# An addition ahead of each indirect transfer of the first retention stage, and the keys' half sums moved from GpSimd to VectorE

## The reference

```python
h = tok(x, conv_w)                 # each token's three rows of a table of 8000 x 3 x 128, one for each tap;
                                   # the taps are added with shifts by one token
h = h + retention(layernorm(h))    # xpos-rotated queries and keys, decay mask, group norm, 8 heads
h = h + experts(layernorm(h))      # 8 experts, each token goes to its best two
h = h + complex_retention(layernorm(h))
h = h + merged_ffn(layernorm(h))
```

## Time and profile before

| | us |
|---|---|
| median of three runs (2256.82 to 2259.97) | 2257.84 |
| the profiled execution | 2260.11 |
| its span, first to last instruction | 2258.1 |
| TensorE busy, share of the span | 2006.5, 89% |
| VectorE | 1469.5, 65% |
| ScalarE | 1340.2, 59% |
| GpSimd | 1123.3, 50% |
| mean granted TensorE clock | 0.937 |

### The profile page before, as it was taken

One profiled execution on the slowest core, in us unless ns is written; L12 is line 12 of the kernel. 1 busy time (PEld: TensorE's weight loads), 2 busy tenths in 40 slices (PEclk: granted clock), 3 DMA queues, 4 the chain that ended last, 5 costly groups with the idle time before them and its releaser, 6 DMA issues. The chain is left out here.

```text
span 2258.1 us, 57460 instructions
## 1 busy us (share of the span) xinstructions
PE 2006.5 (89%) x19420; PEld 1513.2 (67%) x19420; DVE 1469.5 (65%) x4372; ACT 1340.2 (59%) x2844; POOL 1123.3 (50%) x1242
## 2 busy tenths in 40 slices
PE   4888878878878759999999968999999799999997
PEld 2555545555555547777777755777777589999997
DVE  3766666766767533333333337999999668888877
ACT  3655655555556322222222217999999589988985
POOL 4466566566555458887787862112112014333434
PEclk9998998989889769999999988999999899999999
DMA  2111111112111035555555641311110001111111
GB/s 80 55 54 54 58 55 55 55 54 60 51 53 47 29 105 167 166 163 163 161 160 158 164 136 49 132 41 37 46 37 28 6 25 39 44 39 39 39 48 39
DMA packets 113820, 168.88 MB, mean 75 GB/s; under 512 B 19235, under 2 KB 66748, under 8 KB 113573
## 3 DMA queue, kind: packets, MB, share of 16 engines
q1 hardware_dynamic: 87940, 105.22, 16.6%
q0 software_dynamic: 25760, 62.09, 8.6%
HBM read 121.92 MB, written 45.32 MB: 74 GB/s over the span
## 5 line engine op out<-in xcount | busy, mean ns | idle before, releaser
L344 POOL DMA_INDIRECT sent<-a_xn_mid,a_pos_cur x256 | 250.8, 980 | 94.1 <-issue 72.5
L1252 ACT ACTIVATE b_hT<-b_hbank,b_w 128x512 f32<-128x512 f32 (+1 forms) x156 | 98.3, 630 | 320.1 <-PE b_hbank L1222 267.3
L1196 POOL DMA_INDIRECT done<-b_y,b_row x270 | 264.2, 979 | 48.1 <-issue 43.7
L1232 PE MATMUL b_bank<-b_w,b_hT 128*128 128x128 f32 x2160 | 254.2, 275 | 0.9 <-DVE b_hT L1278 0.9
L1278 DVE TENSOR_SCALAR b_hT<-b_hbank,b_w 128x512 f32<-128x512 f32 (+1 forms) x156 | 105.7, 677 | 226.6 <-PE b_hbank L1222 206.4
L1232 PEld LDWEIGHTS b_bank<-b_w,b_hT 128*128 128x128 f32 x2160 | 247.5, 192 | 1.1 <-DVE b_hT L1278 1.1
L1222 PE MATMUL b_hbank<-b_xT,b_w 128*128 128x512 f32 (+1 forms) x624 | 247.2, 539 | 0.8 <-ACT b_xT L1259 0.8
L1485 POOL TENSOR_TENSOR c_k_early<-c_xn,c_k_decay 64x512 f32<-64x512 f32 x32 | 40.8, 1276 | 340.2 <-ACT c_xn L1692 340.2
L450 PE MATMUL a_bank<-a_wkkv,a_xT 128*128 128x384 f32 x256 | 122.4, 563 | 98.0 <-issue 86.3
L744 DVE TENSOR_TENSOR a_masked<-a_scores,a_tabs 128x1024 f32<-128x1024 f32 x128 | 154.7, 1220 | 45.9 <-remote 26.8
L1222 PEld LDWEIGHTS b_hbank<-b_xT,b_w 128*128 128x128 f32 x624 | 113.4, 192 | 87.5 <-issue 83.1
(11 more groups left out here) (245 smaller groups left out, 4728.9 us busy)
## 6 DMA issues: line engine op xcount, KB each, us to landing
b_w<-pack_dram SPq DMA_DIRECT2D x78, 258.0 KB
b_w<-pack_dram SPq DMA_DIRECT2D x78, 256.0 KB
c_rows<-done SPq DMA_DIRECT2D x32, 512.0 KB, 3.9
b_x<-sent SPq DMA_DIRECT2D x57, 260.0 KB
d_b_all<-b_rows SPq DMA_DIRECT2D x32, 256.0 KB, 3.4
out_dram<-h_all SPq DMA_DIRECT2D x32, 256.0 KB, 2.3
b_b<-pack_dram SPq DMA_DIRECT2D x78, 64.5 KB
tv<-tv_dram SPq DMA_DIRECT2D x1, 4736.0 KB, 16.0
```

What stands on the lines that cost most here:

```text
L344: pool.indirect_dma_start(out=sent_d, out_offset=bass.IndirectOffsetOnAxis(ap=pos_cur[:, g.par, b, k:k + 1], axis=0), in_=xn_mid[:, g.par, ...
L1196: pool.indirect_dma_start(out=done_d, out_offset=bass.IndirectOffsetOnAxis(ap=row[:, s.k, j:j + 1], axis=0), in_=y[:, s.par, j, :], in_off ...
L1232: m = nc.tensor.matmul(y_bank[s.par][:, j * D:(j + 1) * D], hT[:, c, j * P:(j + 1) * P], w[:, s.par, W2 + c * D:W2 + (c + 1) * D], start=( ...
```

## The change

Three edits, all of them in `retention_phase`:

1. Each indirect transfer of the stage, gather or scatter, gets a small addition ahead of it on GpSimd: x + x into x, for 128 x 128 words of a stripe of `tv`, the buffer for a table that is loaded in a later stage and is set to zero here. Each addition waits for the one before by a semaphore (`pool_step` for scatters, `ids_step` for gathers; the copy of the indices counts on the latter too).
2. `k_sum` moves from GpSimd, where it stood between the gathers and the scatters, to VectorE, between `place_tokens` and the third mask. Its size and inputs stay. `q_sum` stays on GpSimd.
3. The `sem_inc` of `pool_step` at the head of each group's scatters goes; at the end GpSimd waits for the last addition of each chain.

```diff
@@ retention_phase, gpsimd
             def gather(g):
                 p = g.par
-                pool.wait_ge(ids_ready, g.n + 1)
+                pool.wait_ge(ids_step, g.n * (GB + 1) + 1)
                 if g.is_past(2):
                     pool.wait_ge(h_ready, g.n - 1)
                 take_ids(g.after())
                 for b in range(GB):
+                    space_out(spare[:, 1, :], ids_step, g.n * (GB + 1) + (b + 2))
                     pool.indirect_dma_start(
             def scatter(g, parts):
-                if 0 in parts:
-                    pool.wait_ge(placed, g.n + 1)
-                    pool.sem_inc(pool_step)
                 for i in parts:
                     b, k = divmod(i, 2)
+                    if i == 0:
+                        pool.wait_ge(placed, g.n + 1)
+                    space_out(spare[:, 0, :], pool_step, g.n * (2 * GB) + (i + 2))
                     pool.indirect_dma_start(
-            def k_sum(g):
-                pool.wait_ge(krot_ready, g.n + 1)
-                if g.is_past(1):
-                    pool.wait_ge(kcen_ready, g.n)
-                pool.tensor_tensor(kx[:], kv[:, g.par, :, 0:D], kv[:, g.par, :, D:2 * D], ALU.add).then_inc(kx_ready, 1)
+            def space_out(x, step, n):
+                pool.wait_ge(step, n)
+                pool.tensor_tensor(x, x, x, ALU.add).then_inc(step, 1)
@@ gpsimd, step
                 if g := s.at(3):
                     gather(g)
-                if g := s.at(1):
-                    k_sum(g)
                 if g := s.at(-2):
-                    scatter(g, range(0, GB))
+                    scatter(g, range(GB))
+            pool.memset(spare, 0.0).then_inc(pool_step, 1)
@@ vector
+            def k_sum(g):
+                dve.wait_ge(krot_ready, g.n + 1)
+                if g.is_past(1):
+                    dve.wait_ge(kcen_ready, g.n)
+                v.tensor_tensor(kx[:], kv[:, g.par, :, 0:D], kv[:, g.par, :, D:2 * D], ALU.add).then_inc(kx_ready, 1)
@@ vector, step
                 if g := s.at(-2):
                     place_tokens(g)
+                if g := s.at(1):
+                    k_sum(g)
                 if g := s.at(0):
                     mask(g, 1, 0)
@@ build
+            spare = tv[:, 0:2, :]
```

More of the change, by code:

```diff
@@ L122, in retention_phase @@
 def retention_phase(nc, h_all, w_all, routing, sent_d, ids_d, table_d, wq_d, wqs_d, wkkv_d,
-                    gn_w_d, gn_b_d, tabs_d, tabs_c_d, gate_w_d, gate_c_d, slot_c_d, tags_d):
+                    gn_w_d, gn_b_d, tabs_d, tabs_c_d, gate_w_d, gate_c_d, slot_c_d, tags_d, spare):
     with ExitStack() as ctx:
@@ L235, in retention_phase @@
         consts = sem("consts")
-        ids_ready = sem("ids_ready")
+        ids_step = sem("ids_step")
         tok_made = sem("tok_made")
@@ L321, in take_ids @@
                 pool.tensor_copy(cur_ids[:, g.par * GB:(g.par + 1) * GB],
-                                 ids[:, bass.ds(g.n * GB, GB)]).then_inc(ids_ready, 1)
+                                 ids[:, bass.ds(g.n * GB, GB)]).then_inc(ids_step, 1)
             def gather(g):
                 p = g.par
-                pool.wait_ge(ids_ready, g.n + 1)
+                pool.wait_ge(ids_step, g.n * (GB + 1) + 1)
                 if g.is_past(2):
@@ L367, in step @@
                     gather(g)
-                if g := s.at(1):
-                    k_sum(g)
                 if g := s.at(-2):
-                    scatter(g, range(0, GB))
+                    scatter(g, range(GB))
             pool.memset(ids[:, NB:], 0).then_inc(pool_step, 1)
+            pool.memset(spare, 0.0).then_inc(pool_step, 1)
             pool.wait_ge(ids_loaded, 16)
-            pool.wait_ge(pool_step, 1)
+            pool.wait_ge(pool_step, 2)
             take_ids(Group(0, 0, 0))
@@ L379, in _ @@
                 pool.wait_ge(scattered[i], (NG // 2) * (2 * GB) * 16)
+            pool.wait_ge(pool_step, NG * (2 * GB) + 2)
+            pool.wait_ge(ids_step, NG * (GB + 1) + 1)
         @block.tensor
@@ L2954, in build @@
                        routed.enter_context(nc.sbuf_tensor("ident_b", [P, P], F32)))
+            spare = tv[:, 0:2, :]
             retention_phase(nc, h_all, w_all, routing, sent, a["ids"].bitcast(U32), a["table"], a["wq"],
                             a["wqs"], a["wkkv"], a["gn_w"], a["gn_b"], a["tabs"], a["tabs_c"], a["gate_w"],
-                            a["gate_c"], a["slot_c"], a["tags"])
+                            a["gate_c"], a["slot_c"], a["tags"], spare)
             experts_phase(nc, routing, sent, done, a["pack"], a["fill_tags"])
```

## The result

The changed kernel takes **2198.68 us** in the median (2195.18 to 2203.28), beside 2257.33 of the kernel before in the same comparison: ratio 0.9739, 95% interval 0.9719 to 0.9759. It is faster, as forecast, but 38.7 us above the predicted 2160, and just above the range's end of 2198. The profiled execution spans 2197.6 us, 60.5 less than before. All of it lies in the first stage: the MEMSET that opens the next one stood at 821.59 and stands at 760.4 now.

A forecast was written before the change was run, and what follows sets the result against it. A chain between engines, lengthened by late TensorE signals, was taken to bound the 23.74 us step; 20.4 us a step saves 90, the tail 8, the head 0: 98 off 2260.1 gives 2162, median 2160 us, range 2136 to 2198.

The forecast's parts named there:

- the hold: First retention stage: TensorE's signals arrive late while GpSimd issues indirect transfers in a row; removal taken as -5.0 us a step.
- The rival by which the spaced transfers still hold (2334): First stage: spacing does not break the hold, gate's signal comes later, +2.8 us a step, 2334 us; chance 0.06.
- The chain without holds with k_sum on VectorE: Full step's chain between engines: 23.74 less 5.0 gives 18.7, plus 0.7 for k_sum, 19.4 us.
- The term for k_sum itself: k_sum on VectorE, counted on the chain's path: +0.7 us a step.
- GpSimd's own step: GpSimd in a full step: twelve spaced transfers at 1.54 us plus 1.55 for q_sum, copy and gaps, 20.0 us.
- two other limits near: Full step: the chain's 19.4 and the ring's 20.3 us beside GpSimd's 20.0, so 20.4 was taken.
- The rival with 0.21: First stage: GpSimd's additions and VectorE's two-input operations block each other, 21.3 us a step, 2184 us, up to 2198; chance 0.21.
- What was late next: Full step after the change: GpSimd becomes the bound at 20.0 us, the chain right under it at 19.4.
- The ring of tok and gathers: First stage: a gather is read by tok one step later; 40.6 us for two steps, 20.3 each.
- Tail and head: Ends of the first stage: tail net -8 us (0 to -14), head net 0 (-2 to +1).
- The signs by which I meant to tell: Profile afterwards: gate sum's wait under 1.5 us if right; q_sum 21 us or more apart, spacers much over 0.37 if wrong.
- The half clock: TensorE granted 0.50 of its clock from 408.06 to 414.89 us, mid-step; to be gone or shorter afterwards.

The follow-up runs named there:

- chip B: One of the four chips of the follow-up runs: the kernel before took 2272.71 us there, the changed kernel 2197.61.
- chips A and D: Two of the four follow-up chips: the kernel before took 2108.52 and 2111.84 us on the first, 2107.77 on the second, where the changed kernel took 2200.54.
- k_sum-only kernel: The kernel before with k_sum moved to VectorE and no additions: 2117.03 us (ratio 1.0041) on chip A, 2229.03 (0.9851) on chip C.
- chip B's pair: Changed kernel plus one 1024-column VectorE operation a step: addition with two SBUF inputs 2218.10 us, reduction with one 2203.28, beside 2197.61.
- the k_rotate cut short: Changed kernel with k_rotate on VectorE cut from 1024 columns to 32: 2180.08 us, beside the changed kernel's 2200.54 on chip D.
- chip C: One of the four follow-up chips: the kernel before took 2258.35 us there; the changed kernel was not run on it.

## Why the prediction came out as it did

**The bound and the hold: right, on the chips that have it.** The wait before the gate sum was to fall from 4.2 to the undisturbed 0.8 us a step; it is 0.84. "Remote" waits are gone, and neither the masks nor the sum that closes the retention (L815, now L822) has a wait left among the listed ones (1.0 and 0.9 us a step before). The rival by which the spaced transfers still hold (2334) is refuted by the 0.13 us above, and by the other 26 gates with it. What the hold costs was sized right: 5.0 us a step and 12 in the tail make 27 x 5.0 + 12 = 147 us, and the kernel before takes 146 to 150 us less on chips without it (2257.8 - 2107.8 = 150.0, 2257.8 - 2111.8 = 146.0); against chip B's 2272.7 it is up to 165. The sum took it for the kernel's property, which no single trace could contradict. So the forecast that the change is faster was right for a kind of chip and not for the kernel, and that the result was timed on the kind of chip that the trace came from was luck: on chips A and D the same reasoning would have met a slowdown.

**The chain without holds with k_sum on VectorE: right.** 19.4 us forecast, 19.27 in the k_sum-only kernel on chip A (about 19.0 at its median time, which is 6.4 us under the profiled one). The term for k_sum itself was too high: 0.7 a step, while that kernel is 8.5 us slower than before, 0.3 a step.

**GpSimd's own step: the step that failed.** It was 12 x 1.54 + 1.55 = 20.0, taken as 20.4 with two other limits near; it is 21.83. The timeline of one step shows both parts of the error (GpSimd, 393 to 416 us, the rows that differ and some that don't):

```profile
393.38 1.27 POOL L359 TENSOR_TENSOR a_qx<-a_qa,a_qb 128x512 f32<-128x512 f32 x1
...
394.86 0.40 POOL L353 TENSOR_TENSOR tv<-tv 128x128 f32<-128x128 f32 x1
...
400.10 1.77 POOL L333 DMA_INDIRECT a_rows<-table_dram,a_cur_ids  x1 [0.16 <-issue]
401.89 0.56 POOL L353 TENSOR_TENSOR tv<-tv 128x128 f32<-128x128 f32 x1
...
403.64 0.41 POOL L353 TENSOR_TENSOR tv<-tv 128x128 f32<-128x128 f32 x1
404.22 1.00 POOL L345 DMA_INDIRECT sent<-a_xn_mid,a_pos_cur  x1 [0.17 <-issue]
405.24 0.65 POOL L353 TENSOR_TENSOR tv<-tv 128x128 f32<-128x128 f32 x1
...
407.08 0.41 POOL L353 TENSOR_TENSOR tv<-tv 128x128 f32<-128x128 f32 x1
...
408.67 0.41 POOL L353 TENSOR_TENSOR tv<-tv 128x128 f32<-128x128 f32 x1
...
410.83 1.26 POOL L345 DMA_INDIRECT sent<-a_xn_mid,a_pos_cur  x1 [0.17 <-issue]
...
415.30 1.28 POOL L359 TENSOR_TENSOR a_qx<-a_qa,a_qb 128x512 f32<-128x512 f32 x1
```

Undisturbed, a spaced scatter goes from 407.08 to 408.67, 1.59 us, and a spaced gather, not shown, 1.55 to 1.57 in the same step. I had 1.54, from the experts' addition of 192 columns and a slope of 0.0023 us a column; that slope came from the 512 columns of q_sum, and the addition takes 0.41, not 0.38. With q_sum and the copy at 394.86 - 393.38 = 1.48 the undisturbed step is 8 x 1.59 + 4 x 1.56 + 1.48 = 20.4, **0.4 over** the sum.

The rest is VectorE's. In this step the fourth gather takes 1.77 us instead of 0.96, one scatter 1.26 instead of 0.99, two additions 0.65 and 0.56 instead of 0.41, together 1.47; over all steps the means give 12 x (0.466 - 0.410) = 0.67 for the additions and 8 x (1.020 - 0.979) + 4 x (1.054 - 0.965) = 0.68 for the transfers (0.965 is the gathers' mean in the kernel before; 0.979 in the earlier trace rows). **1.35 us a step**. 20.4 + 1.35 = 21.8. The base of the scatters can be taken otherwise: from the 0.99 that an undisturbed one takes in this step it is 1.27 instead of 1.35, and q_sum's waits for VectorE, 3.1 us in 24 steps, are the 0.13 that is then left. VectorE's rows at the long ones show what ran:

```profile
399.71 1.32 DVE L776 TENSOR_TENSOR a_kv<-a_kv,a_tabs 128x1024 f32<-128x1024 f32 x1
...
401.51 0.68 DVE L792 TENSOR_TENSOR a_kx<-a_kv 128x512 f32<-128x512 f32 x1
...
404.96 0.68 DVE L802 SCALAR_TENSOR_TENSOR a_kcen<-a_ksum,a_kx 128x512 f32<-128x512 f32 x1
...
410.46 0.77 DVE L816 TENSOR_TENSOR a_kn<-a_kcen,a_krs 128x512 f32<-128x512 f32 x1
```

k_rotate starts at 399.71, the gather at 400.10, and it ends 0.84 us after k_rotate's end at 401.03, nearly a gather's whole 0.96, as if it had begun in earnest only then. k_sum, which the change itself brought to VectorE, runs to 402.19 and covers the start of the addition at 401.89, 0.15 too long. k_center starts at 404.96 and the addition at 405.24 is 0.24 too long. The scaling of the keys, 410.46 to 411.23, covers the start of the long scatter at 410.83. The operations named have two inputs in SBUF. That each meeting is the cause of its delay is read from these overlaps; that VectorE's operations of this kind set GpSimd's lengths is shown by chip B's pair and by the k_rotate cut short, which moved 0.4 and 0.66 us of the step. VectorE pays too: k_rotate's mean is 1354 ns over these steps and 1210 with additions of 64 columns, where the meetings fall otherwise:

```profile
L776 DVE TENSOR_TENSOR a_kv<-a_kv,a_tabs 128x1024 f32<-128x1024 f32 x28 | 37.9, 1354 | 0.0
```

```profile
L776 DVE TENSOR_TENSOR a_kv<-a_kv,a_tabs 128x1024 f32<-128x1024 f32 x29 | 35.1, 1210 | 0.0
```

(the first row is the changed kernel's, the second that of the 64 columns on chip D)

**The rival with 0.21 was the mechanism, with too small a price.** It gave each addition 0.07 us by meetings (0.9 a step, 21.3) and named k_rotate, k_center, the scaling and k_sum. Additions came out at 0.056 each, so that estimate was fair. What it missed is that the transfers themselves, 1.0 us long and two thirds of GpSimd's time, meet VectorE as well, for as much again. Forecast 2184 to 2198; measured 2198.7. Its argument against itself, that L1814's median is untouched, was weak: there 61 additions of GpSimd stand beside its 128 executions in 400 us, so most of them can meet none. The Trainium skill, SBUF — State Buffer, Who interferes with whom, states the rule (two SBUF inputs on VectorE against a reading GpSimd instruction, the second blocks). The additions agree with it in kind: those of 0.65 and 0.56 us instead of 0.41 end 0.25 and 0.26 us after the operation of VectorE that they meet, which is less than a whole addition. On the transfers it says that a tensor_tensor was not seen to stall DMA, and infers why; here gathers behind k_rotate took 1.77 instead of 0.96 and cutting k_rotate brought their mean from 1056 to 1005 ns, more than halfway to the 965 of the kernel before, so by the measurement they are stalled, the indirect ones of this kernel at least. Whether it is their reading of the indices or something else that waits was not separated.

**What was late next: right in kind.** GpSimd is the bound. The ring of tok and gathers shows as TensorE's 2.5 us a step of waiting, but it adds nothing of its own: GpSimd's instructions and its waits for VectorE make up the 21.83, and it waits for TensorE nowhere.

**Tail and head: near.** 60.5 us less in the span, 27 x (23.74 - 21.83) = 51.6 of them from the full steps, so 8.9 from both ends, against the 8 forecast. **The sum with the measured step**: 2160 + 27 x (21.83 - 20.4) = 2198.6, and 2198.7 was measured, so the whole miss lies in that one term. **The range** had its upper end at that rival's worst case and should have held more, since both mis-sized terms pushed the same way.

**The signs by which I meant to tell**: an addition much over 0.37 and q_sum 21 us or more apart were named as those of the shared port, and both are there. The half clock went from the gate and came back at tok in the step shown, which I had not foreseen.

## What to carry to other kernels

Before engine A's work is lengthened to relieve a wait, price its new step with the meetings it will have on shared ports for its whole busy time, transfers included, not for the added instructions alone: here that was 1.35 us of 21.8, half as much again as estimated. A stall that the profile gives no releaser for can belong to the chip: run the kernel before on several chips ahead of tuning against it, since this change is worth -2.6 to -3.3% on one kind of chip and +4.2% on the other. And size such a spacer by trial, on a chip that shows the stall: a sixteenth of the length did as well there, and on a chip without the stall any addition only costs, the shorter the less.

## What the runs showed of the hardware that I had not expected

- TensorE's semaphore signals came 3.65 us late (kernel before) during indirect transfers issued in a row on some chips; the k_sum-only kernel shows up to 5.05 us on chip C and at most 0.13 on chip A between 90 and 640 us, with the same instructions. The kernel before takes 2107.8 to 2111.8 us on two of them and 2257.3 to 2272.7 on the others, while the changed kernel takes 2197.6 to 2200.5 on chips of both kinds. What differs between those chips was not found.
- The length of what stands between the transfers counts, not only that something stands there: additions of 0.41 us ended the hold, additions of 0.20 us left 49 of some 150 us. A scatter drawn out from 0.97 to 1.44 us went with an earlier signal in 19 of 19 runs.
- A GpSimd indirect transfer that starts while VectorE runs an operation with two SBUF inputs can get longer: 1.77 us instead of 0.96 beside k_rotate.
- Additions of GpSimd of 8, 32, 64 and 128 columns take 0.21, 0.25, 0.30 and 0.41 us in the median; the means (0.25, 0.34, 0.38, 0.47) hold their meetings with VectorE.
